# Second norm turned by transposing transfers, output projection as three fp16 products of halves, first norm on ScalarE

## What is computed

```python
x = layernorm(h)
xn = x / max(norm(x), eps) * g
u, v, base = split(silu(xn @ uv_w))                 # 256, 256, 128 wide
q, k = base * gamma[0] + beta[0], base * gamma[1] + beta[1]
kern = square(relu((q @ k.T + w_rel) / sqrt(128)))  # 229 x 229 per image
h = h + x * res_scale + (u * (kern @ v)) @ o_w      # the output projection
x2 = layernorm(h)                                   # the second norm
logits = x2 @ gate_w.T + gate_b                     # 8 experts, the best 2 are taken
h = h + shared_experts(x2) + sum(cw * expert(x2))   # 2 shared, 2 of 8 routed, 512 wide
```

## Time and profile before

| | |
|---|---|
| median of 3 runs | 1212.78 us |
| profiled execution, as run | 1205.45 us |
| its span, first to last instruction | 1203.7 us |
| mean granted TensorE clock | 0.992 |
| PE (TensorE matmul) busy | 1158.8 us, 96% |
| DVE (VectorE) busy | 972.5 us, 81% |
| ACT (ScalarE) busy | 806.5 us, 67% |
| POOL (GpSimd) busy | 844.1 us, 70% |
| DMA | 143.51 MB, mean 119 GB/s |

### The profile page before, as it was taken

How to read it: one execution, slowest core, us unless ns; L and a number is a source line. 1 busy time by engine, 2 the same in 40 slices (tenths; PEclk the granted TensorE clock), 3 DMA queues, 4 the chain that set the end, 5 groups by cost and what they waited for, 6 DMA issues and landing times.

```text
span 1203.7 us, 31970 instructions
## 1 busy us (share of the span) xinstructions
PE 1158.8 (96%) x9446; PEld 874.6 (73%) x9446; DVE 972.5 (81%) x2516; ACT 806.5 (67%) x1867; POOL 844.1 (70%) x808
## 2 busy tenths in 40 slices
PE   7999999999999999979989999999999999999998
PEld 4777777777777777845545559999999999965555
DVE  5788998888888888888967777777777777779997
ACT  2566666666765666746545547777777777768887
POOL 5446776666677777678877846777777777776664
PEclk9999999999999999989999999999999999999999
DMA  7233444444444442234344324454444554549998
GB/s 216 71 122 118 126 122 136 135 136 126 129 138 143 134 136 83 88 101 102 105 119 130 98 47 99 98 98 100 92 97 99 92 97 90 92 86 198 207 194 171
DMA packets 208055, 143.51 MB, mean 119 GB/s; under 512 B 119036, under 2 KB 186745, under 8 KB 207892
## 3 DMA queue, kind: packets, MB, share of 16 engines
q1 hardware_dynamic: 166868, 93.93, 31.0%
q0 software_dynamic: 36992, 40.97, 15.8%
q10 hardware_dynamic: 4032, 6.57, 2.2%
HBM read 70.38 MB, written 55.96 MB: 105 GB/s over the span
## 4 chain that ended last, share of the span: by engine, by line
POOL 39%; issue 25%; PE 24%; DVE 4%; ACT 3%; DMA 2%; SPq 1%; POOLq 0%; ACTq 0%; DVEq 0%
POOL y_dram L1645 9%; POOL slots_dram L490 9%; POOL slots_dram L1634 6%; POOL rstd L531 4%; POOL rstd L537 3%; POOL slots_dram L500 3%; PE bank L1929 2%; PE bank L1953 2%; PE bank L1952 2%; PE bank L1954 2%; PE bank L1931 2%; PE bank L1930 2%; POOL emb L460 2%; PE bank L1394 2%; PE bank L1396 2%
## 5 line engine op out<-in xcount | busy, mean ns | idle before, releaser
L1645 POOL DMA_INDIRECT y_dram<-y_sb,y_row x244 | 268.7, 1101 | 92.8 <-issue 73.5
L1728 ACT ACTIVATE gel_all<-bank,b 128x256 f32<-128x256 f32 x488 | 191.8, 475 | 36.6 <-PE bank L1931 33.9
L1361 ACT ACTIVATE gel_all<-bank,b 128x458 f32<-128x458 f32 x256 | 154.9, 640 | 91.1 <-PE bank L1355 63.5
L1952 PE MATMUL bank<-w_part_hi,hid_all 128*128 x976 | 170.6, 219 | 0.0
L1954 PE MATMUL bank<-w_part_hi,hid_all 128*128 x976 | 169.7, 219 | 0.0
L1953 PE MATMUL bank<-w_part_lo,hid_all 128*128 x976 | 169.7, 219 | 0.0
L1850 DVE CAST hid_all<-gel_all 128x1024 f16<-128x1024 f32 x122 | 85.2, 698 | 93.6 <-ACT gel_all L1728 93.6
L490 POOL DMA_INDIRECT slots_dram<-row_bufs,slot_1st x128 | 131.9, 1031 | 40.6 <-issue 38.2
L1852 DVE TENSOR_TENSOR hid_all<-gel_all,hid_all 128x1024 f16<-128x1024 f32 x122 | 149.5, 1226 | 4.2
L1372 DVE TENSOR_TENSOR hid_all<-gel_all,hid_all 128x916 f16<-128x916 f32 x128 | 142.4, 1113 | 4.4
L1634 POOL DMA_INDIRECT slots_dram<-row_bufs,slot_2nd x96 | 119.4, 1243 | 29.9 <-issue 28.7
(11 more groups left out here) (193 smaller groups left out, 3003.3 us busy)
## 6 DMA issues: line engine op xcount, KB each, us to landing
xin<-in_xmain SPq DMA_DIRECT2D x32, 771.8 KB
x2r_dram<-row_bufs SPq DMA_DIRECT2D x32, 260.0 KB, 2.1
x2t_dram<-x2T SPq DMA_DIRECT2D x32, 229.0 KB, 2.9
x_cols<-x2t_dram ACTq DMA_DIRECT2D x28, 229.0 KB
row_bufs<-x2r_dram SPq DMA_DIRECT2D x24, 260.0 KB, 2.9
stage<-in_ffn_w SPq DMA_DIRECT2D x20, 256.0 KB
xin<-in_xrest SPq DMA_DIRECT2D x32, 128.6 KB
y_dram<-y_sb,y_row POOLq DMA_INDIRECT x244
```

What stands on the lines that cost most here:

```text
L1361: act.activation(self.gel[:, f // 2 % 2, f % 2, :], self.up_dst(k, f), ACT.Gelu, bias=self.b1[:, f:f + 1]).then_inc(self.gel_ready, 1)
L1645: pool.indirect_dma_start(out=y_dram, in_=y_sb[:, s, c, :], in_offset=None, out_offset=bass.IndirectOffsetOnAxis(ap=y_row[:, s, c:c + 1], ...
L1728: act.activation(gel[:, s8 % 2, f, :], up_bank[s8 % 2][half][:, (f % 2) * TILE:(f % 2 + 1) * TILE], ACT.Gelu, bias=of_expert(b1, SHARED * ...
L1952: pe.matmul(part, h_hi, w2_hi, start=False, stop=False)
```

## The change

- `CHUNKS` becomes 112 and 117. A pair's columns are laid out with room for 240 columns an image (`IMG_COLS`), 480 a pair.
- The second norm is no longer turned by TensorE. SP issues four transposing transfers from row_bufs (both halves, 256 fp16 columns; 112 or 128 rows each) to x2T16 (`turn_x2`), and stores x2T16 a step later (`store_columns`). `x2_columns`, `columns_hi` and `x2_low` go.
- The logits are computed one step later, at the place where `x2_columns` stood, and into tr2_bank. `top` and `choose` move with them, ahead of the scores; `mx8` has two buffers, `keep_top` runs a step later.
- The output projection: uav is split into uav16 (`gated_hi` on ScalarE, `gated_low` on VectorE), o_w into ow16, and `project` is twelve fp16 products an image instead of four fp32 ones.
- `front_norm` moves from VectorE to ScalarE, with a shift that VectorE makes (`xn_shift`).
- ScalarE's order in a step: the high halves of the gate stand around `second_norm` and `halves_hi`, then `front_norm`, then the SiLU of u.
- At the end of the attention more pieces of shared experts stand between the stages, up to pair 2; the exponentials of the second choice follow pair 2. The shared experts read their columns as two pieces of 229 (`up`).

```diff
-CHUNKS = ((0, 117), (117, 112))
+CHUNKS = ((0, 112), (112, 117))
...
+IMG_COLS = CHUNKS[1][0] + P
+PAIR_COLS = 2 * IMG_COLS
+TURN_ROWS = (CHUNKS[0][1], P)
 PAIR_PATCHES = 2 * PATCHES
...
-
+            def turn_x2(b, parity, buf):
+
+                if reaches(b, 2):
+                    sp.wait_ge(lg_done, b - 1)
+                    sp.wait_ge(t_out[parity], 8 * (b - parity))
                 sp.wait_ge(rows_ready, b + 1)
+                for img in range(2):
+                    for c, (at, _) in enumerate(CHUNKS):
+                        n, col = TURN_ROWS[c], img * IMG_COLS + at
+                        sp.dma_start(x2T16[:, parity, :, col:col + n], rows_16[0:n, buf, 2 * img + c, 0:2 * HID],
+                                     transpose=True).then_inc(x2_turned[parity], 16)
                 sp.dma_start(x2r_dram[b], rows_1st[:, buf]).then_inc(r_out[buf], 16)
-                sp.wait_ge(t_ready, b + 1)
+
+            def store_columns(b, parity):
+
+                sp.wait_ge(x2_turned[parity], 64 * (b // 2 + 1))
                 sp.dma_start(x2t_dram[b], x2T16[:, parity].bitcast(FP32).rearrange("p h n -> p (h n)")
...
                 if 0 < i < WBLOCKS:
                     load_w(i)
+                if exists(i - 2):
+                    store_columns(i - 2, p)
                 if exists(i - 1):
-                    store_x2(i - 1, 1 - p, (q - 1) % 4)
...
-                if i < PAIRS and exists(i - 2):
-                    keep_top(i - 2)
+                if exists(i - 3):
+                    keep_top(i - 3)
                 if exists(i - 4):
                     scatter_rows(i - 4, j - 2, q)
...
                                          op0=ALU.mult, op1=ALU.mult).then_inc(shift_ready, 1)
+                dve.wait_ge(scl_ready, n + 1)
+                dve.scalar_tensor_tensor(out=xn_shift[:, :], in0=mv[:, :, 0], scalar=-1.0, in1=scl[:, :],
...
+            def gated_low(i, img):
+
+                dve.wait_ge(uav_hi, 2 * i + img + 1)
+                dve.tensor_tensor(uav16[:, img, 1], uav[:, img], uav16[:, img, 0], ALU.subtract).then_inc(uav_split, 1)
...
             def top(b, parity):
                 dve.wait_ge(lg_done, b + 1)
-                if not (isinstance(b, int) and b == 0):
-                    dve.wait_ge(top_kept, b)
-                dve.tensor_tensor(lgs[:, :, :], tokb_bank[:, LOGITS_AT:LOGITS_AT + 4 * EXPERTS].rearrange("p (c e) -> p c e", c=4),
+                if reaches(b, 2):
+                    dve.wait_ge(top_kept, b - 1)
+                dve.tensor_tensor(lgs[:, :, :], tr2_bank[:, LOGITS_AT:LOGITS_AT + 4 * EXPERTS].rearrange("p (c e) -> p c e", c=4),
...
                     assemble(2, 0)
+                if exists(i):
+                    gated_low(i, 0)
+                if exists(i - 2):
+                    top(i - 2, p)
+                if p == 1 and exists(i - 3):
+                    choose(j - 1)
                 if exists(i - 1):
-                    x2_low(i - 1, 1 - p)
+                    halves_low(i - 1, (q - 1) % 4)
+                if exists(i):
+                    gated_low(i, 1)
                 for img in range(2):
                     if exists(i + 1):
                         scores(i + 1, img)
                 if exists(i + 2):
                     xnT_low(i + 2, p)
-                if exists(i - 1):
-                    top(i - 1, 1 - p)
-                if exists(i - 1):
-                    halves_low(i - 1, (q - 1) % 4)
-                if p == 0 and exists(i - 2):
-                    choose(j - 1)
...
+            def front_norm(n, parity):
+
+                act.wait_ge(shift_ready, 2 * n + 2)
+                if reaches(n, 1):
+                    act.wait_ge(tr2_done, n)
+                for c in range(4):
+                    last = act.activation(xn[:, c, :], hn[:, parity, c, :], ACT.Identity,
+                                          bias=xn_shift[:, c:c + 1], scale=scl[:, c:c + 1])
+                last.then_inc(xn_ready, 1)
+
+            def gated_hi(i, img):
+
+                act.wait_ge(uav_ready, 2 * i + img + 1)
+                act.activation(uav16[:, img, 0], uav[:, img], ACT.Copy).then_inc(uav_hi, 1)
...
             def step(i, p, j, q):
                 if exists(i + 1):
                     uv(i + 1, 1 - p, 0)
+                if exists(i):
+                    gated_hi(i, 0)
                 if exists(i - 1):
                     second_norm(i - 1, (q - 1) % 4)
-                    if not drains(i):
-                        columns_hi(i - 1, 1 - p)
+                    halves_hi(i - 1, (q - 1) % 4)
+                if exists(i):
+                    gated_hi(i, 1)
+                if i >= 0 and exists(i + 2):
+                    front_norm(i + 2, p)
                 for k in again_begins(i):
...
             def logits(b, parity):
                 if not reaches(b, 1):
-                    pe.wait_ge(uvw_ready, 3)
-                pe.wait_ge(t_ready, b + 1)
-
...
+                    pe.wait_ge(uvw_ready, 4)
+                pe.wait_ge(x2_turned[parity], 64 * (b // 2 + 1))
+
+                pe.wait_ge(xnT_ready, min(b + 4, PAIRS))
                 if reaches(b, 1):
                     pe.wait_ge(lg_read, b)
...
+                    for c, (at, _) in enumerate(CHUNKS):
                         q = 2 * img + c
-                        hi_at = img * SEQ + at
-                        lo_at = PAIR_SEQ + hi_at
-                        lo_n = min(P, 2 * PAIR_SEQ - lo_at)
-                        hi, lo = halves[:, hi_at:hi_at + P], halves[:, lo_at:lo_at + lo_n]
-                        dst = tokb_bank[:, LOGITS_AT + q * EXPERTS:LOGITS_AT + (q + 1) * EXPERTS]
+                        col = img * IMG_COLS + at
+                        hi, lo = x2T16[:, parity, 0, col:col + P], x2T16[:, parity, 1, col:col + P]
+                        dst = tr2_bank[:, LOGITS_AT + q * EXPERTS:LOGITS_AT + (q + 1) * EXPERTS]
                         pe.matmul(dst, hi, gate16[:, 0, :], start=True, stop=False)
                         pe.matmul(dst, hi, gate16[:, 1, :], start=False, stop=False)
-                        last = pe.matmul(dst[0:lo_n, :], lo, gate16[:, 0, :], start=False, stop=True)
+                        last = pe.matmul(dst, lo, gate16[:, 0, :], start=False, stop=True)
                 last.then_inc(lg_done, 1)
 
...
             def project(i, img):
-                pe.wait_ge(uav_ready, 2 * i + img + 1)
+                pe.wait_ge(uav_split, 2 * i + img + 1)
+                if img == 0 and not reaches(i, 1):
+                    pe.wait_ge(uvw_ready, 2)
                 if img == 0 and reaches(i, 1):
                     pe.wait_ge(mid_ready, i)
                 for c, (at, rows) in enumerate(CHUNKS):
...
                     for e in range(2):
-                        last = pe.matmul(o_bank[0:rows, q * HID:(q + 1) * HID], uav[:, img, e, at:at + rows],
-                                         ow[:, e, :], start=e == 0, stop=e == 1)
+                        hi, lo = (uav16[:, img, h, e, at:at + rows] for h in range(2))
+                        pe.matmul(dst, hi, ow16[:, 0, e, :], start=e == 0, stop=False)
+                        pe.matmul(dst, hi, ow16[:, 1, e, :], start=False, stop=False)
+                        last = pe.matmul(dst, lo, ow16[:, 0, e, :], start=False, stop=e == 1)
                 if img == 1:
```

More of the change, by code:

```diff
@@ L1229, in step @@
                     av(i, 1)
-                if exists(i - 1) and not drains(i):
-                    x2_columns(i - 1, (q - 1) % 4)
+                if exists(i - 2) and i != PAIRS - 2:
+                    logits(i - 2, p)
                 if exists(i + 3) and p == 1 and i != -1:
@@ L1254, in step @@
                         rank(j - 1)
-                    logits(i - 1, 1 - p)
+                    else:
+                        logits(i - 2, p)
                     return
@@ L1706, in pair @@
                     early.load(act, i + 2, i % 2)
+            pair(2)
+            act.wait_ge(centred, 2)
+            act.activation(expd, expd, ACT.Exp).then_inc(exps, 1)
+            for parity in range(2):
+                act.wait_ge(done.t_out[parity], 16 * PAIRS // 2)
             act.wait_ge(tags_up, 1)
             tag_rows(0, 0)
[L1710 removed]
+            for i in range(3, EARLY_PAIRS):
                 pair(i)
@@ L1791, in pair @@
                 vector_pair(dve, i, parity)
-            for j in range(2):
-                early.split(dve, 1, 1, j)
+            early.split(dve, 1, 1, NJ - 1)
+            pair(2, 0)
             dve.wait_ge(done.top_kept, PAIRS)
```

209 lines of the change are left out of this document (95 added, 114 removed).

## The result

The changed kernel takes 1218.72 us (median of 20 runs), the kernel before 1209.38 in the same place (20 runs): ratio 1.0072, 95% interval 1.0056 to 1.0089. It is **slower** by 0.7%; the prediction was 6.7 us faster. In the profiled executions the span goes from 1203.7 to 1216.4 us.

What follows compares the result with a forecast made beforehand. TensorE's queue was taken to bound the attention steps, ScalarE's order the odd ones after the change. Start +1.5, steps -2.7 and 0, end -2.5 and -3 gave -6.7 us: median 1206.1, own range 1200 to 1211, overall 1190 to 1222.

Steps and rivals of the forecast that it cites:

- The steps: Attention: odd step 16.7 us, even 14.15, a pair 30.85 instead of 31.14; steps 1 to 18 save 2.7 us.
- the last four: Attention steps 19 to 28: GpSimd's 30.0 to 31.3 us a pair leaves no room, so 0 gained.
- The fp16 projection: Attention steps: twelve fp16 products take 0.70 us instead of 0.87, saving 0.17 on each projection.
- rival 2: Output projection: exposed weight loads make it 1.09 us instead of 0.70; +10 us in total, 1223; chance 0.17.
- rival 3: Transposing transfers over 10.5 us from ready rows to landing; at 12 us +35 us, 1248; chance 0.08.
- The start: Before the attention: ScalarE's slower first norm moves xn's transposes from 24.69 to 25.6; with added weight splits +1.5 us.
- I count 3 us less idle time: End of attention: wider maxima buffer and filler cut TensorE's wait for the last ranks; -3 us, between 0 and 6.
- shifts by +1.5 - 2.7 - 0.3 = -1.5: GpSimd's scatter chain up to the routed tiles: it comes 1.5 us earlier, tile 0 landing by 708.5.
- 4.9 of issue and 2 of landing: Last logits, end of attention: four transposing transfers cost this after ready rows, instead of 2.6 us through TensorE.
- the slack: Start of routed tiles: tile 0 may land by 710, TensorE begins it at 716.25, so TensorE is last by 6 us.
- later stages only shift: Behind the attention: shared products in two pieces and the bias product keep their pace; no term in the sum.
- Rival 4: Attention steps: ScalarE's chain 0.5 us longer; odd steps +0.5, even +0.3, 14 pairs +11 us, 1217; chance 0.17.

Runs made afterwards that it cites:

- e5b: The changed kernel with the first norm back on VectorE; 1.0098 of the kernel before, beside the changed kernel's 1.0125.
- e25: The changed kernel with pair 31 turned by TensorE, its routing ahead of the filler, and the first norm back on VectorE; 1.0068 of the kernel before.
- e2b: The changed kernel with pair 31 alone turned by TensorE and its routing ahead of the filler; 1.0044 of the kernel before, beside the changed kernel's 1.0125.
- a2: The changed kernel with 19 instead of 18 shared-expert pairs ahead of the routed tiles; 0.9992 of the kernel before, repeated at 0.9967, on slower chips.
- b1: The kernel before with GpSimd delayed by eight idle powers (10.9 us) ahead of pair 30's scatter; ratio 1.0048, repeats 1.0081 and 1.0055, on slower chips.
- e25c: The changed kernel with pair 31 turned by TensorE, routing before filler, first norm on VectorE, 19 early shared-expert pairs; 0.9867, 0.9890, 0.9895, on slower chips.

## Why the prediction was wrong

**The steps came out, in part by luck.** Predicted 30.85 for a pair, measured 30.67. But the odd step is 16.12 and not 16.7, the even one 14.55 and not 14.15, and the two errors cancel. The mechanism is the predicted one: a wait near 1 us for the text copy, measured 1.70, and TensorE without idle time ahead of the logits. From the patches of step 2 to those of step 28 it takes 3.1 us less, with -2.7 predicted: 4.5 less in the first nine pairs of steps and 1.5 more in the last four, for which 0 was predicted. The fp16 projection takes 0.67 us, predicted 0.70; rival 2 (exposed weight loads, 1.09) is dead. So is rival 3, late transfers: four of them take 5.04 us of issue, where 4.9 was the most reckoned with, and even for the last pair it is 8.7 us from the first issue to the logits, under the 10.5 that it needed.

**The start was mis-sized.** Predicted +1.5. The first xn's transposes move by 27.66 - 24.69 = 2.97. Of this, 1.6 lies ahead of the norm (VectorE makes the scale at 24.89 instead of 23.32): 0.8 is a transfer that ScalarE's set-up waits for (16.17 instead of 15.40), 0.4 the splitting of o_w, and 0.4 the transposes of hT, which take 1.07 us instead of 0.67 at a falling clock. The other 1.4 is the path of the norm through ScalarE and VectorE's extra shift. In e5b and e25 they start at 25.85 and 24.96.

**The step that failed is the end, "I count 3 us less idle time", and with it GpSimd's chain, which "shifts by +1.5 - 2.7 - 0.3 = -1.5".** Its start at the end of the attention was put at -0.3, which no row supports; it measured +11.2 at the scatter of pair 30 (553.04 against 541.81) and +12.2 at tile 0. I priced the last logits at 4.9 of issue and 2 of landing (no row was given for the landing, which took 3.7), and then let filler cover them. The filler does cover TensorE. But in the kernel before the slots were ready 1.9 us before GpSimd needed them, at the start of a chain of 162 us with no gap of over 0.9 us in it. Filler on TensorE covers nothing there; it stands in the way. What the runs showed in place of -3: VectorE's last middle 3.0 later, with two projections waiting for their halves and then running at half clock, where I had it 2.1 earlier by this alone; from norm to logits 13.2 us, of it 2.93 for a buffer whose scatter came late, 5.04 of issue and 3.7 from there to the first product; 4.0 for ranks behind filler. e2b took out the turn and the filler for the last pair alone and got 6 to 10 us back; how much each of the two gives on A is not shown.

**The second failure is the slack, and "later stages only shift".** "So TensorE's chain is last by 6 us" took the time between tile 0 and its first product as free. In the changed kernel the tile lands 4.25 us after TensorE is ready (722.26 - 4.25 = 718.01, where 709.5 was predicted and the kernel before has 716.25). So 6.0 of the 12.7 us of the profiled execution are there at the first product, 6.3 more come in the tiles and 0.4 behind them. Of the 6.3, 3.6 are idle time of TensorE (5.1 against 1.5) and 2.7 are longer busy time; a part of that is the half clock behind the wait, where products of 256 columns start 0.21 us apart instead of 0.11 until 725.6. That the lost lead is what costs the idle time fits four of the five traces without a lead; e5b, with 0.8 us of waits behind the first tile, does not need it. The experiments made for it, a2 and b1, met only chips where they can't show it. It stays the best reading, not a proof.

Rival 4 (slower, ScalarE's chain) had the right sign and nearly the right time, 1217, for a wrong reason: the steps didn't lengthen by the 0.8 us a pair that it needed.

No version beats the kernel before on A: the best are e2b at 1.0044 and e25 at 1.0068. So at least 0.4% of the loss has no experiment that removes it. In B e25c is 1.1 to 1.3% under the kernel before; it has not run on A.

## What to carry to other kernels

Before covering a latency with filler, look for the engine whose gapless queue begins with that result, and compare when the result is ready with when it is needed: here 539.87 against 541.81, a hand-over with 1.9 us to spare. What comes later than that arrives at the end of the queue. The releaser of a row inside the engine's usual pause tells when the result came, not how much it had to spare: e2b has the same "<-DVE slot_1st" in a pause, 3.6 us before the slots are needed. Time between the first load of a stream and its first use should not be booked as slack when loads come nearly at the rate of use: in these traces it looks like what absorbs late ones. And a transfer that is free in the steady state, where a whole step hides 5 us of issue and 4 of landing, is paid in full for the last item: try turning that one the old way.

## What the runs showed of the hardware

- Four transposing transfers of 112 or 128 rows of 256 fp16 cost SP 5.04 us to issue, 1.26 each, as much as one of 256 rows from DRAM: fewer rows saved nothing. From the end of issue to the logits it took 3.7 us.
- fp16 products of 128 columns with weights of 112 or 117 columns follow each other every 0.056 us (12 in 0.67), as with 128 columns: the 35 ns longer weight load does not show.
- Chips differ by 16 to 19% in this program and in the sign of this change: 0.995 in B, 1.0072 and 1.0125 on A. In B TensorE stops for about 1.2 us again and again with no releaser in the profile. What makes it stop stays open.
- TensorE's granted clock is at the lower level, 1.2 GHz, behind waits of 2.7 to 4.3 us: 0.51 behind 3.01 us in step 29, 0.50 behind 2.72 us in step 31, 0.55 from 722 to 725 behind 4.25 us.
- GpSimd's fill of a 128x5120 buffer takes 4.39 us, and a cast of 128x916 on VectorE that starts beside it takes 4.91 instead of 0.63; in the changed kernel the fill (4.38 us at 716.36) falls where VectorE has nothing to do, and no cast is caught.
